# Row maxima of attention scores: negated and transposed by VectorE in 32 by 32 blocks instead of by TensorE and ScalarE

## What is computed

```python
x = x + tanh(g_xattn) * xattn(layernorm(x), ctx, ctx, mask)   # 16 heads of 16, biases, softmax over keys
x = x + tanh(g_ffn) * moe(layernorm(x))                        # 8 experts, each takes its 1024 best tokens
# inside xattn
scores = where(mask == 0, -1e9, Qh @ Kh^T / sqrt(10)); probs = softmax(scores); out = probs @ Vh
```

## Time and profile before

| | |
|---|---|
| median of the runs | 817.03 us |
| the profiled execution | 819.81 us, its span 818.1 us |
| busy: PE, PEld, DVE, ACT, POOL | 756.5, 632.5, 563.9, 512.8, 367.5 us |
| L1145 transposes on PE | 64, 277 ns each |
| L579 negations on ACT | 64, 249 ns each |
| L369 copies on SP | 64, 8.0 KB each |
| L750 maxima on DVE | 256, 684 ns each |

### The profile page before, as it was taken

The page is one execution under the profiler, slowest core; times in us unless marked ns, Lnnn a source line. Parts: engine busy times, 40 slices in busy tenths (PEclk is TensorE's granted clock), DMA queues, the critical chain, the costliest instruction groups (busy, mean ns, idle before and its releaser), DMA issues. The chain is left out here.

```text
span 818.1 us, 24964 instructions
## 1 busy us (share of the span) xinstructions
PE 756.5 (92%) x9638; PEld 632.5 (77%) x9638; DVE 563.9 (69%) x1451; ACT 512.8 (63%) x1001; POOL 367.5 (45%) x760
## 2 busy tenths in 40 slices
PE   9999999999999999999998514899999999999995
PEld 5778888888888888888877402778889898888985
DVE  7777778777877787778777797574655747464440
ACT  4366777777777777777667673546555555646632
POOL 5324453445343534354413312527365474747415
PEclk9999999999999999999999855999999999999998
DMA  7444434554355444544233270435446263524314
GB/s 232 129 127 132 147 127 129 171 173 151 115 160 173 141 139 148 175 144 141 77 114 103 72 215 25 159 91 85 110 80 120 64 139 116 87 43 86 34 19 52
DMA packets 76773, 97.08 MB, mean 119 GB/s; under 512 B 8264, under 2 KB 55880, under 8 KB 76616
## 3 DMA queue, kind: packets, MB, share of 16 engines
q1 hardware_dynamic: 63120, 77.52, 29.5%
q0 software_dynamic: 12288, 17.05, 12.7%
q10 hardware_dynamic: 1248, 0.92, 0.3%
HBM read 52.37 MB, written 25.72 MB: 95 GB/s over the span
## 5 line engine op out<-in xcount | busy, mean ns | idle before, releaser
L750 DVE TENSOR_REDUCE m_sb<-a_ps 128x4 f32<-128x512 f32 x256 | 164.4, 684 | 52.4 <-PE a_ps L1063 51.0
L572 ACT ACTIVATE p_t<-b_ps 128x512 f32<-128x512 f32 x252 | 141.7, 589 | 67.3 <-PE b_ps L1071 64.9
L1063 PE MATMUL a_ps<-k_st,q_st 31*128 31x128 f32 x2048 | 148.6, 282 | 6.9 <-DVE m_sb L750 2.7
L1487 POOL DMA_INDIRECT out<-y,idx_add x64 | 100.4, 1569 | 116.8 <-ACT y L1548 95.6
L1063 PEld LDWEIGHTS a_ps<-k_st,q_st 31*128 31x128 f32 x2048 | 124.8, 186 | 31.8 <-issue 22.1
L1071 PE MATMUL b_ps<-q_st,k_st 32*128 32x128 f32 x1984 | 143.8, 283 | 0.0
L484 POOL TENSOR_TENSOR x<-o_n,x_res 128x256 f32<-128x256 f32 x63 | 46.1, 732 | 186.8 <-DVE o_n L840 167.8
L1071 PEld LDWEIGHTS b_ps<-q_st,k_st 32*128 32x128 f32 x1984 | 120.2, 186 | 0.0
L1748 DVE TENSOR_TENSOR act_h<-act_h,bank 128x512 f32<-128x512 f32 x64 | 44.0, 688 | 81.3 <-PE bank L1892 73.9
L1892 PE MATMUL bank<-x_hi,w_hi 128*128 128x512 f32 x248 | 97.6, 393 | 0.2 <-issue 0.2
L1892 PE MATMUL bank<-x_lo,w_hi 128*128 128x512 f32 x248 | 96.6, 390 | 0.0
(11 more groups left out here) (305 smaller groups left out, 1743.6 us busy)
## 6 DMA issues: line engine op xcount, KB each, us to landing
w<-in_w_t SPq DMA_DIRECT2D x24, 512.0 KB
rows_scratch<-xg SPq DMA_DIRECT2D x16, 528.0 KB, 3.5
x_in<-in_x SPq DMA_DIRECT2D x16, 512.0 KB, 4.8
c_t<-in_ctx_t SPq DMA_DIRECT2D x16, 512.0 KB, 4.2
k_st<-k_val SPq DMA_DIRECT2D x64, 128.0 KB
q_st<-q_val SPq DMA_DIRECT2D x64, 128.0 KB, 2.3
x_res<-in_x SPq DMA_DIRECT2D x16, 512.0 KB, 3.9
out<-x SPq DMA_DIRECT2D x16, 512.0 KB, 3.2
```

The lines of the kernel that those rows point to most:

```text
L572: act.activation(p_t[b.s % 2][:, 4 * r:4 * r + 4, :], ps[q % 2][:].rearrange("p (h s) -> p h s", s=P), ACT.Exp, scale=SCALE).then_inc(exp_ ...
L750: dve.tensor_reduce(m_sb[b.s % 2][:, 4 * q:4 * q + 4], a_ps[q % 2][:].rearrange("p (h s) -> p h s", s=P), AX_X, ALU.max).then_inc(max_done, 1)
L1063: mm = pe.matmul(a_ps[i][:, t * P:(t + 1) * P], q_st[p][r:r + A_K, t, tok], k_st[p][r:r + A_K, t, tok], start=True, stop=True)
L1487: pool.indirect_dma_start(out[:, :], bass.IndirectOffsetOnAxis(ap=idx_add[e % 2][:, st:st + 1], axis=0), y[st][:], None, compute_op=ALU.ad ...
```

## The change

VectorE's reductions write the maxima already negated, into `m_sb` of 128 by 32 (the 16 columns beyond the heads are zeros, set once). Behind the fourth maximum of a batch VectorE waits for its own four reductions (and for the copies that last read this `neg_m`, two batches ago) and runs one transpose, which turns each 32 by 32 block by itself: the maxima of tokens 32i to 32i+31 come to lie in partitions 32i to 32i+15 of `neg_m`, 128 by 32. `max_rows` then sends four DMAs, one for each block, of 16 rows of 32 numbers. TensorE's `max_t`, ScalarE's `negate` and the waits `m_free` are gone; `scores` waits for 64 counts of `s_m`, four DMAs of 16.

```diff
@@ -194,8 +194,8 @@
     k_st = [sb(f"k_st{p}", [P, TILES, GT]) for p in range(2)]
     v_aug = [sb(f"v_aug{p}", [P, GB, HEADS, VW]) for p in range(2)]
 
-    m_sb = [sb(f"m_sb{i}", [P, HEADS]) for i in range(2)]
-    neg_m = [sb(f"neg_m{i}", [HEADS, P]) for i in range(2)]
+    m_sb = [sb(f"m_sb{i}", [P, RG]) for i in range(2)]
+    neg_m = [sb(f"neg_m{i}", [P, RG]) for i in range(2)]
     p_t = [sb(f"p_t{i}", [P, HEADS, P]) for i in range(2)]
     o_t = [sb(f"o_t{i}", [P, 4, P]) for i in range(2)]
     o_n_last = sb("o_n_last", [P, D])
@@ -366,7 +366,10 @@
             def max_rows(b):
                 if b.ok:
                     sp.wait_ge(neg_done, b.times(1, 1))
-                    sp.dma_start(q_st[b.group.p][MAX_ROW:P:RG, :, b.j * P:(b.j + 1) * P], neg_m[b.s % 2][:]).then_inc(s_m[b.s % 2], 16)
+                    for i in range(P // RG):
+                        at = b.j * P + i * RG
+                        sp.dma_start(q_st[b.group.p][MAX_ROW:P:RG, :, at:at + RG],
+                                     neg_m[b.s % 2][i * RG:i * RG + HEADS, :]).then_inc(s_m[b.s % 2], 16)
 
             def store_x2(g):
                 if g.ok:
@@ -572,12 +575,6 @@
                     act.activation(p_t[b.s % 2][:, 4 * r:4 * r + 4, :], ps[q % 2][:].rearrange("p (h s) -> p h s", s=P),
                                    ACT.Exp, scale=SCALE).then_inc(exp_done, 1)
 
-            def negate(b):
-                if b.ok:
-                    act.wait_ge(mt_done, b.times(1, 1))
-                    wait(act, s_m[b.s % 2], b.turn(2, 16))
-                    act.activation(neg_m[b.s % 2][:], m_ps[0:HEADS, 0:P], ACT.Copy, scale=-1.0).then_inc(neg_done, 1)
-
             def pv_copy(b, ps=pv_ps):
                 if b.ok:
                     act.wait_ge(pv_done, b.times(1, 1))
@@ -695,7 +690,10 @@
         @block.vector
         def _(dve):
             dve.memset(warm[:], 0.0).then_inc(s_warm, 1)
+            for i in range(2):
+                dve.memset(m_sb[i][:], 0.0).then_inc(s_blank, 1)
             dve.memset(q_st[0][:], 1.0).then_inc(s_ones, 1)
+            dve.wait_ge(s_blank, 2)
 
             def stats(g, ts):
                 if not g.ok:
@@ -746,9 +744,13 @@
                 if b.ok:
                     dve.wait_ge(a_done, b.times(4, q + 1))
                     if q == 0:
-                        wait(dve, mt_done, b.times(1, -1))
+                        wait(dve, neg_done, b.times(1, -1))
                     dve.tensor_reduce(m_sb[b.s % 2][:, 4 * q:4 * q + 4], a_ps[q % 2][:].rearrange("p (h s) -> p h s", s=P),
-                                      AX_X, ALU.max).then_inc(max_done, 1)
+                                      AX_X, ALU.max, negate=True).then_inc(max_done, 1)
+                    if q == 3:
+                        dve.wait_ge(max_done, b.times(4, 4))
+                        wait(dve, s_m[b.s % 2], b.turn(2, 64))
+                        dve.transpose(neg_m[b.s % 2][:], m_sb[b.s % 2][:]).then_inc(neg_done, 1)
 
             def row_scores(g):
                 if g.ok:
@@ -1053,7 +1055,7 @@
                     wait(pe, max_done, b.times(4, 2 * x))
                 if back.ok:
                     if x == 0:
-                        pe.wait_ge(s_m[back.s % 2], back.turn(2, 16, 16))
+                        pe.wait_ge(s_m[back.s % 2], back.turn(2, 64, 64))
                     wait(pe, exp_done, back.times(4, 2 * x))
                 for t in range(TILES):
                     for i in range(2):
@@ -1093,16 +1095,12 @@
                 if q == 3:
                     mm.then_inc(pv_done, 1)
 
-            def m_free(b):
-                use = Batch(b.k, b.s, NB).back(1)
-                if use.ok:
-                    pe.wait_ge(neg_done, use.times(1, 1))
-
             def router(g, b):
                 if g.ok:
                     pe.wait_ge(xt2_out, g.times(2, 2))
+                    if first(g):
+                        pe.wait_ge(s_same, 4)
                     wait(pe, st_out, g.times(1))
-                    m_free(b)
                     for k in range(KD):
                         for t in range(GB):
                             mm = pe.matmul(m_ps[VW * t:VW * (t + 1), R_AT:R_AT + P], wg_sb[:, k, :, :].rearrange("p u e -> p (u e)"), xn2_t[:, k, t * P:(t + 1) * P],
@@ -1130,19 +1126,6 @@
                 for i in range(2):
                     mm = pe.matmul(a_ps[0][:, i * P:(i + 1) * P], ends[:, i:i + 1].to_broadcast([P, P]), ident[:], start=True, stop=True)
                 mm.then_inc(s_bcast, 1)
-
-            def max_t(b):
-                use, g = b.back(1), b.group.on(-3)
-                if use.ok:
-                    if use.k + use.s == 0:
-                        pe.wait_ge(f_free[1], 4)
-                    if b.j == 2 and g.ok:
-                        pe.wait_ge(st_out, g.times(1, 1))
-                    if use.k + use.s == 1:
-                        pe.wait_ge(s_same, 4)
-                    wait(pe, neg_done, use.times(1))
-                    pe.wait_ge(max_done, use.times(4, 4))
-                    pe.transpose(m_ps[0:HEADS, 0:P], m_sb[use.s % 2][:], ident[:]).then_inc(mt_done, 1)
 
             def out_back(use, ps=o_ps):
                 if use.ok:
```

More of the change, by code:

```diff
@@ L243, in attention @@
     a_done, max_done = sem("a_done"), sem("max_done")
-    mt_done, neg_done = sem("mt_done"), sem("neg_done")
+    neg_done, s_blank = sem("neg_done"), sem("s_blank")
     s_m = [sem(f"s_m{i}") for i in range(2)]
@@ L632, in step @@
                 exp(b.back(2), 0)
-                negate(b.back(1))
                 exp(b.back(2), 1)
@@ L673, in _ @@
             steps(act, step)
-            negate(batch(NB - 1))
             xt2_copy(group(NG - 3), 0)
@@ L1169, in last_scores @@
                 if x == 0:
-                    pe.wait_ge(s_m[b.s % 2], b.turn(2, 16, 16))
+                    pe.wait_ge(s_m[b.s % 2], b.turn(2, 64, 64))
                     pe.wait_ge(exp_done, b.times(4))
@@ L1220, in step @@
                 scores(b, 0)
-                max_t(b)
                 if not first(g):
@@ L1246, in _ @@
             edge = batch(NB)
-            max_t(edge)
             pe.wait_ge(f_free[0], 4 * NG)
```

## The result

The changed kernel takes 820.11 us (median of 20 runs, 816.91 to 825.78) against 816.96 us before (20 runs, 815.52 to 819.92). The medians differ by 3.15 us. The ratio of the two kernels is 1.0044, with a 95% interval of 1.0031 to 1.0057, which is 3.6 us slower. Its runs spread over 8.9 us where those of before spread over 4.4. Ratios use fast runs alone: one run of e11 (1484.74 us) and one of the kernel before beside it (874.59 us) are left out as slow.

A forecast was written before the change was run, and what follows sets the result against it. TensorE, busy 99.77 of 100 us in the attention stage, was taken as the bound. Its saving of 1.5 us and 4.9 us for late copies sum to +3.4 on 817.03: 820.4 us, 8-in-10 range 814 to 829.

The forecast's parts named there:

- TensorE's transpose: Removing L1145 on TensorE saves 0.06 us before the token transposes plus 3 x 0.015 before projections, 0.105 us a group.
- The whole saving: TensorE's saving over some 14 groups of attention: 1.5 us, bounds nothing and 7.0 us.
- VectorE's transpose: Added on VectorE behind the fourth maximum: 0.2 us, plus 0.1 for waiting for its own four reductions.
- The cover: Between batches 3 and 0, L718's 0.40 us wait for ScalarE hides VectorE's added 0.3 us; above 0.4, TensorE loses time.
- The tie at 263.21 and 263.43: L718 ends at 263.21, transposes L1021 start at 263.43: exactly on time with 0.2 us for the semaphore.
- SP's queue: Four copies take 2.40 us; x_in moves 1.4 us later, and batch 2's copies behind it keep about 0.5 us of slack.
- The pauses: A usual 1.2 us queue pause before x_in costs TensorE about 0.7 us, in seven of 14 groups: 4.9 us.
- All copies in time: Rival: all maxima copies on SP's queue arrive in time, only TensorE's saving is left: 815.5 us, chance 0.27.
- Late in every group: Rival: maxima rows late ahead of batch 0's scores, 0.7 to 1.1 us in each of 14 groups: 825 to 831 us, chance 0.27.
- VectorE dear: Rival: VectorE's transpose costs 0.64 us plus 0.1, exceeding the cover by 0.35 in 14 groups: 820.4 us, chance 0.05.
- Full spacing of the matmul: Rival: on TensorE the removed matmul and its release cost full spacing everywhere, 7.0 + 1.4 us: 808.6, chance 0.04.
- The end of the stage: Last four copies issued 445.6 to 448.0, landing near 449.5; TensorE's last scores start at 449.56: 0 +- 0.5 us.

The follow-up runs named there:

- e11: Kernel before with its one maxima copy cut into four and the x_in load issued by ScalarE's queue: 821.85 us, ratio 1.0080 to the kernel before.
- e3: Changed kernel with one maxima copy a batch instead of four, leaving out the maxima of 96 tokens: 814.99 us, ratio 0.9967 to the kernel before.
- e6: e3 with its VectorE transpose done twice, the first into a tile nothing reads: 818.85 us, ratio 0.9980 to the kernel before.
- e9: Changed kernel with four 32 x 32 VectorE transposes directly behind the fourth maximum and one copy a batch: 826.43 us, ratio 1.0076 to the kernel before.
- e1: Changed kernel with the x_in load moved on SP's queue from batch 2's step to the end of batch 3's: 816.96 us, ratio 0.9998 to the kernel before.
- e7: Changed kernel with the x_in load issued by ScalarE's DMA queue in the same step: 818.53 us, ratio 0.9981 to the kernel before.
- e2: Kernel before, transpose and negation kept, with its one maxima copy cut into four: 825.25 us, ratio 1.0106 to the kernel before.
- e8: Changed kernel with four 32 x 32 VectorE transposes at the end of VectorE's step and one copy a batch: 823.35 us, ratio 1.0032 to the kernel before.

## Why the prediction was right, point by point

The forecast was 820.4 us, of 14 groups seven late by 0.7 us each. Measured were 820.11 us, and six late by 0.9 us on average (5.1 us). The mechanism was right. That the number fits so closely is in part luck: the saving was taken too small (1.5, 2.7 by e3) and the price of four copies too (4.9, 6.3 by e3 against the change), and the two errors cancel.

- **TensorE's transpose, 0.105 us a group.** Right. Batch 0's scores start at 373.82 and 400.74 in two undisturbed groups of the changed kernel, and at 370.60 and 397.62 before: 26.92 against 27.02 us, 0.10.

```profile
400.74 0.38 PE L1065 MATMUL a_ps<-k_st,q_st 31*128 31x128 f32 x2
```

```profile
397.62 0.38 PE L1063 MATMUL a_ps<-k_st,q_st 31*128 31x128 f32 x2
```

- **The whole saving, 1.5 us.** Too small by about 1 us: e3 shows 2.7 (1.5 to 4.0). By its trace, 1.5 us come from the groups as worked out. Another 1.0 comes at the end. The steps of the last group have no projections, and there the second exponential, which the negation held up, released TensorE in every second half; without the negation VectorE's maxima do, and e3 gains 0.46 us over this group. These are such a half before and in e3:

```profile
442.84 0.38 PE L1063 MATMUL a_ps<-k_st,q_st 31*128 31x128 f32 x2 [0.25 <-ACT p_t L572]
440.86 0.38 PE L1063 MATMUL a_ps<-k_st,q_st 31*128 31x128 f32 x2 [0.35 <-DVE m_sb L746]
```

That makes half of it; the other half comes between this and the last scores, which no longer have `max_t` ahead of them. The prediction counted the copy removed from ScalarE at 0: right for the groups, a term left out for the last one.
- **VectorE's transpose.** 0.2 us taken, 0.211 measured. The Trainium skill's 311 ns for 128 x 128 bf16 ("VectorE: DVE Perf Modes", The three transpose paths) is the 311 ns that 128 x 128 float32 took in e3, so by the trace that figure agrees, though bf16 itself was not run. The cover did not "just about hold", it held with room (e6). The size of the cover, 0.4 us, was the step that was mis-sized: e9's 0.83 us lengthens a group to 27.26 us from 26.92, by 0.34, which puts it at 0.5 to 0.6 with the wait. The tie at 263.21 and 263.43 was taken with 0.2 us for a semaphore; it takes less: in e9 L714 ends at 239.16 + 0.69 = 239.85, and the transposes that wait for it start at 239.91.
- **SP's queue.** The four copies take 2.36 us (2.40 taken), `x_in` moves by 1.40 us (1.4) and lands in 4.9 us. The load's place is what makes the copies late: shown by e1 and e7, in which the same load at another place, or earlier and in another queue, takes the waits from 5.1 to 1.1 and 0.7 us. That they "queue behind the load's 512 KB" is right for their packets, but its transfer makes up only some 2.0 of the 5.1 us; most is the time of the last issue. The four copies behind the load were taken with 2.5 us and take 2.77 in most groups, up to 3.12.
- **The pauses.** Each lateness in the changed kernel stands in a group in which the queue paused before `x_in`. That was the part with the least ground under it, and both profiles of the change have six such waits. The sizes were off, in opposite directions: the load is 0.9 us late on average, not 1.2, and nearly all of that reaches TensorE, where 0.5 us of slack was to take its part; 0.9 - 0.85 leaves 0.05. That the late groups lie in a row was not foreseen. What makes the queue pause is seen only as a coincidence with packets of instructions; it was not tried by itself.
- **The rule against small transfers** ("DMA: Bandwidth & Descriptors", Rules for kernel authors, of the Trainium skill): the trace agrees as far as one copy is better than four by 0.0077 of the ratio (e3 against the change). By e1 to e3, what costs is not how long one small copy takes to land but four turns in a queue that other work shares.
- **The rivals.** All copies in time: 815.5 was given, and e3 gives 815.0. Late in every group: not seen, the worst is e2 with 11 waits, in eight of its groups. VectorE dear: not with one transpose. Full spacing of the matmul: no.
- **The end of the stage**, 0 +- 0.5: right. The profile puts 0.19 us of idle time ahead of the last scores down to the copies, but 0.18 us stand there before the change too, so nothing is lost.

```profile
451.59 0.82 PE L1160 MATMUL b_ps<-q_st,k_st 32*128 32x128 f32 x10 [0.19 <-DMA q_st<-neg_m]
```


## What to carry to other kernels

An operation taken from the bounding engine is worth the distance it puts between its neighbours, which was 0.01 to 0.06 us here for an instruction of 0.28 us. What replaces it must be counted on the queue it goes through: three more DMAs are three more turns on a queue, and what they push back here is a large load, and with it the small urgent copies behind it. Put the load behind such copies, or issue it earlier from another engine, before changing how they are made; and look how long a pause of the queue the place can bear.

## What was not expected of the hardware

- VectorE's transpose costs by instruction more than by size: 199 ns for 32 x 32 (e8), 211 for 128 x 32, 311 for 128 x 128 in float32, and 269 for the second of two in a row (e6).
- SP's queue takes 0.52 us to issue a copy of 2 KB and 0.60 for one of 8 KB in most places, and up to 1.6 us when it pauses (one query copy at 226.85).
- A copy can move its packets late without being late itself: behind the load the first packet comes 3.2 us after the first issue and not 1.9, but the last one 0.76 us after the last issue and not 0.73. Where the load's packets are nearly through by the last issue, its bytes cost next to nothing; in e1, where three loads stand right ahead of the copies, they cost 1.8 us in one group.
